# Gate and up projections of a mixture-of-experts layer as seven block products instead of eight, on one Trainium2 core

## The reference, cut to what matters

```python
# x: (2, 1024, 256); 8 experts, D = 256, F = 1024; one shared expert
g = jnp.einsum('bsd,edf->ebsf', h, Wg)
u = jnp.einsum('bsd,edf->ebsf', h, Wu)
expert_outs = jnp.einsum('ebsf,efd->ebsd', jax.nn.silu(g) * u, Wd)
expert_output = jnp.einsum('be,ebsd->bsd', gating_probs, expert_outs)
shared = jnp.einsum('bsf,fd->bsd', jax.nn.silu(h @ Sg) * (h @ Su), Sd)
x = x + (1.0 - sg) * expert_output + sg * shared
# second layer, short: scores = tanh(x @ W1 + b1) @ v; masked softmax over l; pooled = p @ x / count
x = x + pooled
```

## Time and profile before

| | |
|---|---|
| three timed runs | 1239.90, 1240.72, 1240.99 us (median 1240.72) |
| span of the profiled execution | 1241.5 us |
| TensorE busy | 1232.6 us, 99%, 5409 matmuls |
| VectorE busy | 734.6 us, 59% |
| GpSimd busy | 602.0 us, 48% |
| ScalarE busy | 199.2 us, 16% |
| DMA | 61.07 MB, mean 49 GB/s |

### The profile page before, as it was taken

The page is one execution under the profiler, slowest core; times in us unless marked ns, Lnnn a source line. Parts: engine busy times, 40 slices in busy tenths (PEclk is TensorE's granted clock), DMA queues, the critical chain, the costliest instruction groups (busy, mean ns, idle before and its releaser), DMA issues.

```text
span 1241.5 us, 15497 instructions
## 1 busy us (share of the span) xinstructions
PE 1232.6 (99%) x5409; PEld 1007.1 (81%) x5409; DVE 734.6 (59%) x963; ACT 199.2 (16%) x342; POOL 602.0 (48%) x640
## 2 busy tenths in 40 slices
PE   8999999999999999999999999999999999999998
PEld 7888888888888888888888888888888888887765
DVE  5655655656556565565655656556555565555756
ACT  2111111111111111111111111111111111111222
POOL 6855549596444444444444444444444444443301
PEclk9999999999999999999999999999999999999997
DMA  5111111112111111111111111111111111101001
GB/s 170 54 51 49 38 40 51 51 34 68 51 51 51 51 40 36 50 51 51 51 51 51 51 51 42 35 50 51 51 51 51 51 51 51 48 33 47 1 9 59
DMA packets 63981, 61.07 MB, mean 49 GB/s; under 512 B 4576, under 2 KB 63968, under 8 KB 63968
## 3 DMA queue, kind: packets, MB, share of 16 engines
q1 hardware_dynamic: 63680, 60.90, 15.7%
q10 hardware_dynamic: 288, 0.01, 0.0%
HBM read 58.80 MB, written 2.10 MB: 49 GB/s over the span
## 4 chain that ended last, share of the span: by engine, by line
PE 99%; DVE 0%; DMA 0%; ACT 0%; SPq 0%; issue 0%
PE gate_ps L720 11%; PE acc L720 11%; PE gate_ps L721 11%; PE gate_ps L724 11%; PE acc L724 11%; PE acc L721 11%; PE up_ps L720 10%; PE up_ps L724 10%; PE up_ps L721 10%; PE spare L778 1%; PE acc L820 0%; DMA x_nat<-in_x 0%; PE spare L801 0%; PE acc L825 0%; PE acc L809 0%; PE gate_ps L809 0%
## 5 line engine op out<-in xcount | busy, mean ns | idle before, releaser
L541 DVE SCALAR_TENSOR_TENSOR h<-gate_silu,gates,up_ps 128x512 f32<-128x512 f32 x288 | 215.3, 748 | 455.6 <-PE up_ps L724 455.6
L317 POOL TENSOR_TENSOR wd_hi<-raw_d,zero 128x256 fp32r<-128x256 f32 x144 | 92.1, 639 | 541.0 <-PE acc L724 541.0
L548 DVE TENSOR_TENSOR h_lo<-h,h_hi 128x512 fp32r<-128x512 f32 x288 | 326.1, 1132 | 9.9
L420 ACT ACTIVATE gate_silu<-gate_ps 128x512 f32<-128x512 f32 x288 | 172.4, 599 | 985.0 <-PE gate_ps L724 985.0
L720 PE MATMUL gate_ps<-xT_hi,wgu_hi 128*128 128x512 f32 x576 | 225.0, 391 | 1.3 <-DVE xT_lo L530 1.3
L721 PE MATMUL gate_ps<-xT_hi,wgu_lo 128*128 128x512 f32 x576 | 224.2, 389 | 0.0
L720 PE MATMUL acc<-h_hi,wd_hi 128*128 128x512 f32 x576 | 224.2, 389 | 0.0
L720 PE MATMUL up_ps<-xT_hi,wgu_hi 128*128 128x512 f32 x576 | 224.2, 389 | 0.0
L724 PE MATMUL gate_ps<-xT_lo,wgu_hi 128*128 128x512 f32 x576 | 224.1, 389 | 0.0
L724 PE MATMUL up_ps<-xT_lo,wgu_hi 128*128 128x512 f32 x576 | 224.1, 389 | 0.0
L721 PE MATMUL acc<-h_hi,wd_lo 128*128 128x512 f32 x576 | 224.1, 389 | 0.0
(11 more groups left out here) (118 smaller groups left out, 663.3 us busy)
## 6 DMA issues: line engine op xcount, KB each, us to landing
raw_gu<-in_L_cond_Wg SPq DMA_DIRECT2D x64, 256.0 KB, 2.7
raw_gu<-in_L_cond_Wu SPq DMA_DIRECT2D x64, 256.0 KB, 3.3
raw_d<-in_L_cond_Wd SPq DMA_DIRECT2D x64, 256.0 KB, 3.6
x_nat<-in_x SPq DMA_DIRECT2D x8, 256.0 KB, 6.9
raw_gu<-in_L_cond_Sg SPq DMA_DIRECT2D x8, 256.0 KB, 2.7
raw_gu<-in_L_cond_Su SPq DMA_DIRECT2D x8, 256.0 KB, 3.2
raw_d<-in_L_cond_Sd SPq DMA_DIRECT2D x8, 256.0 KB, 3.7
out_x<-x_nat SPq DMA_DIRECT2D x8, 256.0 KB, 2.1
```

The costliest lines, as they stand in the source:

```text
L317: nc.gpsimd.tensor_tensor(wd_hi[:, f, :], raw_d[:, s, j, :], zero[:, 0:1].broadcast_to([P, D]), ALU.add).then_inc(d_hi_done, 1)
L420: nc.scalar.activation(gate_silu[:, u % 2, :], gate_ps[:], ACT.Silu).then_inc(silu_done, 1)
L541: nc.vector.scalar_tensor_tensor(out=h[:, i, :], in0=gate_silu[:, i, :], scalar=gate_of[:, bass.ds(step, 1)], in1=up_ps[:], op0=ALU.mult, ...
L548: nc.vector.tensor_tensor(h_lo[:, s, :], h[:, i, :], h_hi[:, s, :].bitcast(F32), ALU.subtract).then_inc(h_split, 1)
```

## The change

The first layer is computed for both batches in turn on four tiles of F (a chunk of a routed expert: 4 groups of batch 0, then 4 of batch 1), so that GpSimd splits the weights of the routed experts once and not twice; the shared expert's are still split for each batch. In all 80 tiles are split instead of 144. A ring of six tiles (`RING`) holds the split weights.

Gate and up of a group are one 2x2 by 2x2 block product: the token halves times the D blocks, against the D blocks times (gate, up). Instead of 8 block products there are 7 (Strassen's scheme in Winograd's form), numbered 1 to 7. Their operands are sums: of activation blocks, made once for each batch by `combine_x` on VectorE, rounded by ScalarE (`round_x`) and completed by `rest_x`; and of weight blocks, made for each pair of tiles by GpSimd (`combine`, three instructions). A split instruction of a tile then covers seven blocks instead of four (128x896 elements).

The results need sums too. Products 1 and 2 are added up in PSUM (`g_ps`), with product 1 copied to SBUF between them (`keep_p1`, ScalarE); products 7 and 4 share `e_ps`; 6, 5 and 3 share a bank `v_ps`. Five VectorE additions of a PSUM bank and an SBUF tile make the rest (`keep_p7`, `keep_v`, `second_gate`, `second_up`, `first_up`). The two hidden multiplications (`hidden_first`, `hidden_second`) now read two SBUF tiles, `h_hi` is rounded by ScalarE (`round_h`), and `h_lo` stays on VectorE (`rest_h`). ScalarE goes from two to five instructions in a group. Since `acc` holds one chunk only, `add_acc` adds it to `xT` after each: four more additions per four groups of an expert.

Loops are written out; a group has 33 matmuls instead of 36. TensorE's order in it: products 4, 5, then 1 of the next group, down of the first half, 2 of the next, 3, then 7 and 6 of the next, down of the second half.

The diff, cut to its core:

```diff
+    PAIR = 2
+    RING = 6
+    RAWS = 2
...
+    for e in range(E):
+        for c in range(FT // CHUNK):
+            n0 = len(uses)
+            for f in range(CHUNK):
+                uses.append((e, c * CHUNK + f))
+            for b in range(B):
+                for f in range(CHUNK):
+                    groups.append((b, n0 + f, f == 0, f == CHUNK - 1))
+    for b in range(B):
+        for f in range(FT):
+            uses.append((E, f))
+            groups.append((b, len(uses) - 1, f == 0, f == FT - 1))
...
-                    nc.gpsimd.tensor_tensor(wgu_hi[:, f, w, :], gu[:, w, :],
-                                            zero[:, 0:1].unsqueeze(2).broadcast_to([P, w.stop - w.start, P]),
-                                            ALU.add).then_inc(hi_done, 1)
-                    pool.wait_ge(hi_done, n + 1)
-                    nc.gpsimd.tensor_tensor(wgu_lo[:, f, w, :], gu[:, w, :], wgu_hi[:, f, w, :].bitcast(F32),
-                                            ALU.subtract).then_inc(split, 1)
...
+            def combine(s, cols):
+                w = raw[:, s, :, cols]
+                n = cols.stop - cols.start
+                t_made(nc.gpsimd.tensor_tensor(w[:, 4:6, :], w[:, 1:4:2, :],
+                                               w[:, 0:1, :].broadcast_to([P, 2, n]), ALU.subtract))
+                t_made(nc.gpsimd.tensor_tensor(w[:, 6, :], w[:, 3, :], w[:, 4, :], ALU.add))
+                t_made(nc.gpsimd.tensor_tensor(w[:, 7, :], w[:, 2, :], w[:, 6, :], ALU.subtract))
...
+            def split_tile(n):
...
+                    if n >= RING:
+                        pool.wait_ge(p_done[3], final_group[n - RING] + 1)
+                    elif n >= RING // 2:
+                        pool.wait_ge(xT_done, B * KD * NT)
+                    split(w[:, 1:8, :], hi, lo, NP, gu_hi_done, n + 1, gu_split)
+                split_d(n)
...
+            def keep_p1(i):
+                act.wait_ge(p_done[1], i + 1)
+                if i >= 2:
+                    act.wait_ge(up0_done, i - 1)
+                nc.scalar.activation(p1_sb[:, i % 2, :], g_ps[:], ACT.Copy).then_inc(p1_copied, 1)
...
+            for i in range(NG):
+                gate_second(i)
+                if i + 1 < NG:
+                    keep_p1(i + 1)
+                round_h(1, i)
+                first_bank(i - L1_AT)
+                if i + 1 < NG:
+                    gate_first(i + 1)
+                round_h(0, i)
...
-                nc.vector.scalar_tensor_tensor(out=h[:, i, :], in0=gate_silu[:, i, :],
-                                               scalar=gate_of[:, bass.ds(step, 1)], in1=up_ps[:],
-                                               op0=ALU.mult, op1=ALU.mult).then_inc(h_done, 1)
-                dve.wait_ge(h_done, n)
-                nc.vector.tensor_copy(h_hi[:, s, :], h[:, i, :]).then_inc(h_hi_done, 1)
-                dve.wait_ge(h_hi_done, n)
-                nc.vector.tensor_tensor(h_lo[:, s, :], h[:, i, :], h_hi[:, s, :].bitcast(F32),
-                                        ALU.subtract).then_inc(h_split, 1)
...
+            def keep_p7(i):
+                dve.wait_ge(p_done[7], i + 1)
+                dve.wait_ge(p1_copied, i + 1)
+                if i:
+                    dve.wait_ge(up1_done, i)
+                nc.vector.tensor_tensor(p7_sb[:], e_ps[:], p1_sb[:, i % 2, :], ALU.add).then_inc(p7_copied, 1)
+            def keep_v(i):
...
+                nc.vector.tensor_tensor(v_part[:], v_ps[i % 2][:], p1_sb[:, i % 2, :], ALU.add).then_inc(v_copied, 1)
+            def first_up(i):
...
+                nc.vector.tensor_tensor(up0[:], v_ps[i % 2][:], p1_sb[:, i % 2, :], ALU.add).then_inc(up0_done, 1)
+            def second_gate(i):
...
+                nc.vector.tensor_tensor(gate1[:], e_ps[:], v_part[:], ALU.add).then_inc(gate1_done, 1)
+            def second_up(i):
...
+                nc.vector.tensor_tensor(up1[:], v_ps[i % 2][:], p7_sb[:], ALU.add).then_inc(up1_done, 1)
+            def hidden_second(i):
+                dve.wait_ge(silu1_done, i + 1)
+                dve.wait_ge(up1_done, i + 1)
+                if i:
+                    dve.wait_ge(h_hi_done[1], i)
+                nc.vector.scalar_tensor_tensor(out=h[1][:], in0=silu1[:], scalar=gate_of(i), in1=up1[:],
+                                               op0=ALU.mult, op1=ALU.mult).then_inc(h_done[1], 1)
...
+            def rest_h(t, i):
+                dve.wait_ge(h_hi_done[t], i + 1)
+                nc.vector.tensor_tensor(h_lo[t][:, i % 2, :], h[t][:], h_hi[t][:, i % 2, :].bitcast(F32),
+                                        ALU.subtract).then_inc(h_split[t], 1)
...
+            for i in range(NG):
+                second_gate(i)
+                second_up(i)
+                hidden_second(i)
+                if i >= 2 and groups[i - 2][3]:
+                    add_acc(1, i - 2)
+                rest_h(1, i)
+                if i >= 1 and groups[i - 1][3]:
+                    add_acc(0, i - 1)
+                first_up(i)
+                hidden_first(i)
+                if i + 1 < NG:
+                    keep_p7(i + 1)
+                    keep_v(i + 1)
+                rest_h(0, i)
...
-            def unit(b, u, step):
-                gate(b, u, step)
-                down((u - LAG) % UNITS, step if u >= LAG else step - 1)
-                up(b, u, step)
...
+            def product(q, i, ps, start):
+                b, n = groups[i][:2]
+                if i == first_of_b[b]:
+                    pe.wait_ge(xs_split[b], XQ[q] + 1)
+                hi, lo = weights(n)
+                three_pass(ps[:], hi[:, WQ[q], :], lo[:, WQ[q], :], xs_hi[b][:, XQ[q], :], xs_lo[b][:, XQ[q], :],
+                           start, True).then_inc(p_done[q], 1)
...
+                p4(i)
+                p5(i)
+                if i + 1 < NG:
+                    gate_start(i + 1)
+                if i:
+                    down(0, i - 1)
+                if i + 1 < NG:
+                    gate_end(i + 1)
+                p3(i)
+                if i + 1 < NG:
+                    p7(i + 1)
+                    p6(i + 1)
+                if i:
+                    down(1, i - 1)
```

More of the change, by code:

```diff
@@ L560, in _, with add_acc @@
+            def add_acc(t, i):
+                b = groups[i][0]
+                half = slice(t * BANK, (t + 1) * BANK)
+                dve.wait_ge(down_done[t], i + 1)
+                for d in range(KD):
+                    nc.vector.tensor_tensor(xT[:, b, d, half], acc[d][t][:], xT[:, b, d, half],
+                                            ALU.add).then_inc(acc_read[t], 1)
             counted = [0]
@@ L713, in keep_busy @@
+                        mm.then_inc(xT_done, 1)
             def keep_busy(n):
[L715 to L724 removed]
@@ L738, in gate @@
[L738 to L749 removed]
+                for k in range(n):
+                    nc.tensor.matmul(v_ps[k % 2][:], blank[:, 0:P], blank[:], start=True, stop=True)
@@ L761, in down @@
+            def down(t, i):
+                b, n, first, end = groups[i]
+                if i == first_group[n]:
+                    pe.wait_ge(d_split, n + 1)
+                if first and acc_before[i]:
+                    pe.wait_ge(acc_read[t], KD * acc_before[i])
+                elif first:
+                    pe.wait_ge(xT_copied, B * KD * NT)
+                pe.wait_ge(h_split[t], i + 1)
                 for d in range(KD):
                     cols = slice(d * P, (d + 1) * P)
-                    mm = three_pass(acc[d][t][:], wd_hi[:, f, cols], wd_lo[:, f, cols],
-                                    h_hi[:, u % HS, :], h_lo[:, u % HS, :], start, stop)
@@ L782, in score_row @@
-            def score_row(b):
-                for t in range(NT):
-                    pe.wait_ge(tanh_done, b * NT + t + 1)
-                    nc.tensor.matmul(SCORE[b][t][:], v_rep[:], attnT[:, b, t * BANK:(t + 1) * BANK],
-                                     start=True, stop=True).then_inc(score_done, 1)
+                    mm = three_pass(acc[d][t][:], wd_hi[:, n % RING, cols], wd_lo[:, n % RING, cols],
+                                    h_hi[t][:, i % 2, :], h_lo[t][:, i % 2, :], first, end)
```

856 lines of the change are left out of this document (487 added, 369 removed).

## The result

The changed kernel took 1330.53 us (median of 4 runs, 1327.69 to 1335.58) beside 1240.86 for the kernel before on the same chip: ratio 1.0717, 95% interval 1.0695 to 1.0739. Slower, as forecast, but by 7% and not by 3%: the profiled execution took 1328.73 us, 50 more than the sum of 1278.5, and lies above the range (1190 to 1315).

What follows compares the result with a forecast made beforehand. TensorE's issue alone was taken to bound the kernel before; after, VectorE's port waits take back the 98 us saved. 1241.5 + 10 (routed chunks) + 10 (shared expert) + 12 (head) + 5 (second layer) = 1278.5, forecast 1278 us, range 1190 to 1315.

Steps and rivals of the forecast that it cites:

- the head at +12: Start of the kernel: VectorE's extra pieces for both batches' inputs, plus port waits, add 12 us, between +4 and +22.
- the 7.48 us of products in a group: TensorE in each group: 33 matmuls at the old kernel's 0.2266 us each, 7.48 us instead of 8.16.
- VectorE's additions ahead of product 4: Groups beside a working GpSimd: TensorE waits ahead of product 4 for keep_p7, which stands behind hidden_first.
- VectorE alone 7.0 us: VectorE's work in a group without port waits, one stall for ScalarE's rounding included: 7.0 us, 0.5 under TensorE's 7.48.
- The port, 4 x 0.5 = 2.0 us in 78 groups: Groups beside a working GpSimd: both rests and both hidden multiplications each wait 0.5 us for GpSimd, 2.0 us a group.
- 9.0 us in a busy group: Group beside a working GpSimd: VectorE's 7.0 us plus 2.0 us of port waits, 9.0 us, sets its time.
- The second layer, +5: Batch 0's second layer: 12.0 us of VectorE work in five groups with 0.5 us slack each, +5, between 0 and +12.
- the shared expert's port term (21 us): Shared expert: a tile split in every group, so about 14 of its 16 groups take 9.0 us instead of 7.48.
- the 66.5: Time around the 144 groups in the kernel before (head, second layer, end): 66.5 us, TensorE's own second-layer inserts included.
- only the rests are held: Rival, groups beside GpSimd: hidden multiplications don't take the port; 8.2 to 8.6 us a group, 1216 to 1247 us; chance 0.13.
- VectorE fits after all: Rival, groups beside GpSimd: four port waits together under 0.5 us, so groups stay at 7.48 us; 1156 us; chance 0.18.
- GpSimd itself is last: Rival, GpSimd's splitting: a tile takes 10.5 us instead of 9.1 as both engines hold each other up; 1323 us; chance 0.10.

Runs made afterwards that it cites:

- e1: The changed kernel with GpSimd loading and splitting only the first six weight tiles, which later groups reuse (result not the layer's): 1223.62 us, ratio 0.9861.
- e16: The kernel before with 64 bytes of padding between raw and split weights, so weights and hidden tiles start 64 bytes further, split input unmoved: 1269.93 us.
- e14: The changed kernel with weights, hidden tiles and all behind them aligned to 512 bytes, second batch's split input and product 1's copies 32 bytes off: 1326.16 us.
- e15: The changed kernel with second batch's split input and product 1's copies aligned to 512 bytes, weights, hidden tiles and all behind them 64 bytes off: 1326.05 us.
- e10: The kernel before with 64 bytes of padding behind the transposed input, so split input, weights and hidden tiles all start 64 bytes further: 1242.71 us.
- e5: The kernel before plus two VectorE additions of 128x512 and one ScalarE copy per unit of work, into tiles that nothing reads: 1257.08 us.

## Why the prediction was wrong

The mechanism held: VectorE's additions, held up by the port, set the time of the groups beside GpSimd. The failed steps are terms of the sum around it: the head at +12, which measured +28, and the 7.48 us of products in a group, which measured 7.66. Step by step:

- *What bounds: VectorE's additions ahead of product 4.* Right. L685 was the named releaser, 73 times.
- *VectorE alone 7.0 us.* A little low. In e1, without the port, a group needs 6.25 us of VectorE and 0.70 of waiting for ScalarE's rounding; of the two in four that add `acc`, one needs 7.97 with this wait and the other 7.3 without it. That is 7.3 in the mean, and the group of 7.97 sets its own time.
- *The port, 4 x 0.5 = 2.0 us in 78 groups.* Right in the sum: 150 us held / 78 = 1.93; in time it cost 106 us for the 118 counted. The rule of who is exposed (two SBUF inputs) held for the hidden multiplications, which no row had shown; "Who interferes with whom" in the Trainium skill's page "SBUF — State Buffer" agrees. GpSimd's pieces average 1.83 and 2.40 us for the 1.7 and 2.1 taken, but that is the port again, the other way round: where no held VectorE instruction was still running at their start, they took 1.68 (53 of 79) and mostly 2.08 to 2.12 (10 of 12), and behind one 2.13 and 2.45. A tile's time adds up to 9.3 us in the working and not to 9.1, which changes nothing in the 0.5.
- *7.48 us of products in a group, from 0.2266 each.* This step failed: 7.66. I carried the product's price from one kernel to another as if it belonged to the instruction. It belongs to the operands' places too: 0.232. In e16 the kernel before pays the same price. It is +0.18 in every quiet group, 11 us over 62 of them, and of the 25 us that the experts' groups were over the sum, 12 went when the tiles were aligned.
- *9.0 us in a busy group.* Too small by 0.2: a mean chunk of 8 x 8.44 = 67.5 us less four quiet groups at 7.66 leaves 9.2 for each busy one (8.6, 9.8, 9.1 and 9.0 around 713). After a stall as at 718 the clock could fall as well. Stretches of TensorE behind the same stall of another chunk, and in quiet groups (length, busy us and count, clock, DMA share, GB/s):

```profile
515.20:518.60 3.40, 3.39 (x10) 0.63 0.00 0
736.00:751.00 15.00, 15.00 (x66) 1.00 0.00 1
```

  TensorE had idled 1.87 us up to 515.21. Its next four products started 0.23 to 0.37 us apart, and from 516.39 on eight of them started 0.43 apart, at the lower of the clock's two levels, 1.2 GHz; 77 products between 100 and 1120 us did. At 0.2 us each that is 15 us of issue, an upper bound, since some lie where VectorE is late anyway.
- *The head, +12.* This step failed too, and by the most: +28, above its own range of +4 to +22. The first product came 4.3 us later, and TensorE idled 10.0, 3.6 and 3.3 us ahead of product 4 in groups 0 to 2. Timeline of VectorE in group 0, and of TensorE behind it:

```profile
33.10 2.55 DVE L640 TENSOR_TENSOR s_tmp<-xT 128x512 f32<-128x512 f32 x1
35.58 1.10 DVE L642 SCALAR_TENSOR_TENSOR s_tmp<-xT 128x512 f32<-128x512 f32 x1
36.78 1.02 DVE L646 SCALAR_TENSOR_TENSOR s_tmp<-s_tmp,xT 128x512 f32<-128x512 f32 x1
37.91 1.98 DVE L650 TENSOR_TENSOR s_tmp<-xT,s_tmp 128x512 f32<-128x512 f32 x1
```

```profile
43.02 0.79 PE L911 MATMUL e_ps<-xs_hi,wq_hi 128*128 128x512 f32 x1 [10.03 <-DVE p_sb L685]
```

  Four sums that I priced at 0.65 each took 6.65 us beside a GpSimd that is busy 6.84 of the 7 us from 33 on, and TensorE stood 10.03 us. How much of this is the port and how much the length of the sums themselves no run separates: e1 leaves GpSimd's work of this stretch in place.
- *The second layer, +5, and the end.* Low as well, but hidden: from group 128 on the trace is 6 us above the sum with the port and 12 without it, so the shared expert's port term (21 us) was some 5 too high. In e1 groups 137 to 142 are 15 us longer than quiet ones; 7 of these are TensorE's own inserts, which stood in the 66.5, so that 7 answer to the +5. Another 6.0 us went in front of the block sums, where TensorE waited for `e_diag`, which it didn't before: I had priced VectorE's passes against its slack, but not that `block_weights` is now the last link.
- *The rivals.* That only the rests are held fell (1064 and 942 ns). That VectorE fits after all fell. "GpSimd itself is last" had the nearest number, 1323, by the wrong mechanism: GpSimd waited for a slot once per chunk, 23 us. Of the signs of being wrong one showed, in small: TensorE waited for ScalarE's copy of product 1, twice, 5.0 us in all.

The sign came from the port and was right, though its term was some 10 us too high. The size missed by the head, +16, and the groups of the experts, +25, of which 11 to 12 are the products' price; the rest of these 25 is in the busy groups, with VectorE's 0.3 and the lower clock among its causes, and no run divides it further.

## What to carry to other kernels

When a scheme trades TensorE's products for VectorE's additions, count the slack that remains per group (here 0.5 of 7.5 us) against the longest single GpSimd instruction (2.4 us), not against the mean. Cut GpSimd's instructions before moving anything: four pieces gave 79 us, reordering 26 at most, and a release of GpSimd must not sit on the instruction just ahead of a VectorE pass over two SBUF tiles. An instruction moved to an idle engine waits there in order, for its inputs too, and holds up what stands behind it: ScalarE's 0.94 us cost nothing by themselves, its waits for GpSimd's sums cost 17. And check the start offsets of a product's two operands whenever tiles are laid out anew.

## What the runs showed of the hardware

- Moving operand and weights whose start offsets differ by 64 bytes (e16), and by 32 or 64 (e14, e15), cost 2.4% in the mean of the fp32 products of 128x512, down products between them included: 0.2321 instead of 0.2267 us. A common offset of 64 bytes costs nothing (e10). The Trainium skill's page "SBUF — State Buffer", section "Who interferes with whom", gives the moving operand and the weight load independent ports and says that TensorE waits for no other engine. The latter agrees (e5: 2205 products in 500 us for 2207, with VectorE busy 435 us for 297). The loss by offsets stands beside it: it is measured, and what makes it no run shows.
- A held rest does its work from 0.14 us before GpSimd's instruction ends (100 cases in the changed kernel, 141 before), a held hidden multiplication from 0.21 us before (81 cases).
- ScalarE copies 128x512 and 128x896 from SBUF in 632 and 943 ns; the 1138 that I had worked from are those of 8x1024 with a second input. I had 710 for the first.
- GpSimd's rounding of 128x896 takes 1.68 us where it doesn't start behind a held VectorE instruction, and its rest 2.1; behind one they take 2.13 and 2.45. In pieces of 256 its work costs more in all, 769.4 us busy for 629.3.
